# GpSimd makes the temperature features in iterations 1 to 7; VectorE keeps only their reciprocal

## The reference, cut to what matters

```python
qk = jnp.einsum('bhqd,bhkd->bhqk', Q, K)
scores = qk / math.sqrt(dk)
mean_sim = scores.mean(axis=(-2, -1))
max_sim = scores.max(axis=-1).mean(axis=-1)
probs = jax.nn.softmax(scores, axis=-1)
entropy_proxy = jnp.var(probs, axis=-1, ddof=1).mean(axis=-1)
feats = jnp.stack([mean_sim, max_sim, entropy_proxy], axis=-1)
hidden = jax.nn.gelu(_linear(feats, w1, b1), approximate=False)
hidden = jax.nn.gelu(_linear(hidden, w2, b2), approximate=False)
log_t = jnp.clip(_linear(hidden, w3, b3), LOG_T_MIN, LOG_T_MAX)
t = jnp.exp(log_t)[..., None]
attn = jax.nn.softmax(qk / (2.0 * t), axis=-1)
```

## Time and profile before

| | |
|---|---|
| device time, median of three | 1333.83 us (1332.42 to 1334.48) |
| device time of the profiled execution | 1336.35 us |
| its span | 1334.5 us, 23561 instructions |
| PE / DVE / ACT / POOL busy | 1186.8 (89%) / 1093.2 (82%) / 941.7 (71%) / 396.3 us (30%) |
| mean granted clock of TensorE | 0.969 of full speed |

### The profile page before, as it was taken

How to read it: one execution, slowest core, us unless ns; L and a number is a source line. 1 busy time by engine, 2 the same in 40 slices (tenths; PEclk the granted TensorE clock), 3 DMA queues, 4 the chain that set the end, 5 groups by cost and what they waited for, 6 DMA issues and landing times.

```text
span 1334.5 us, 23561 instructions
## 1 busy us (share of the span) xinstructions
PE 1186.8 (89%) x6684; PEld 439.0 (33%) x6684; DVE 1093.2 (82%) x2049; ACT 941.7 (71%) x1593; POOL 396.3 (30%) x387
## 2 busy tenths in 40 slices
PE   4866598989999999998999999999989899869988
PEld 2322221444134422444124431344214441224234
DVE  7789689896998869896998869897898979985256
ACT  4688598576985689575985669665985669765833
POOL 3138555311452024510353124510353101100120
PEclk9969799999999999999999999999999999979989
DMA  8722211221112221211112221102112210001000
GB/s 305 224 75 64 55 41 49 48 48 58 35 39 48 57 74 48 49 38 42 50 48 48 55 76 49 28 21 65 64 49 48 48 65 1 1 0 47 18 0 32
DMA packets 36049, 73.70 MB, mean 55 GB/s; under 512 B 8144, under 2 KB 8528, under 8 KB 35408
## 3 DMA queue, kind: packets, MB, share of 16 engines
q1 hardware_dynamic: 35920, 72.13, 18.8%
HBM read 38.39 MB, written 8.39 MB: 35 GB/s over the span
## 4 chain that ended last, share of the span: by engine, by line
PE 49%; DVE 26%; issue 10%; ACT 8%; SPq 2%; DMA 1%; DVEq 1%; ACTq 0%; POOL 0%; POOLq 0%
PE b_ps L1445 10%; DVE stat L1017 7%; PE o_ps L1685 6%; DVE nmax L1007 5%; PE o_ps L1490 4%; ACT region L810 4%; PE o_ps L1445 4%; PE b_ps L1477 4%; PE a_ps L1471 4%; PE z_ps L1445 3%; ACT etile L778 2%; DVE hmax L1218 2%; PE z_ps L1685 2%; PE z_ps L1501 2%; PE b_ps L1650 2%
## 5 line engine op out<-in xcount | busy, mean ns | idle before, releaser
L778 ACT ACTIVATE etile<-a_ps,nmax 128x512 f32<-128x512 f32 x512 | 369.1, 734 | 104.3 <-DVE nmax L1007 104.1
L810 ACT ACTIVATE region<-b_ps,inv2t 128x512 f32<-128x512 f32 x512 | 354.8, 758 | 50.0 <-PE b_ps L1477 46.1
L1007 DVE TENSOR_REDUCE nmax<-a_ps 128x1 f32<-128x512 f32 x512 | 345.9, 679 | 53.7 <-PE a_ps L1471 49.7
L1017 DVE BATCH_NORM_STATS2 stat<-etile 128x6 f32<-128x512 f32 x492 | 335.5, 685 | 15.5 <-ACT etile L778 15.2
L1471 PE MATMUL a_ps<-kst,qst 96*128 96x512 f16 x512 | 198.1, 390 | 32.1 <-ACT etile L778 25.5
L1477 PE MATMUL b_ps<-qst,kst 97*128 97x512 f16 x512 | 192.8, 389 | 23.6 <-DVE region L1244 7.7
L1490 PE MATMUL o_ps<-region,vbuf 128*32 128x512 f32 x1024 | 137.2, 608 | 10.9 <-ACT region L810 7.1
L1477 PEld LDWEIGHTS b_ps<-qst,kst 97*128 97x128 f16 x512 | 49.2, 96 | 290.4 <-ACT region L810 259.3
L1501 PE MATMUL z_ps<-region,ones 128*32 128x512 f32 x1024 | 136.2, 604 | 8.4 <-DVE region L1054 8.4
L684 POOL TENSOR_TENSOR region<-region 128x512 f16<-128x512 f32 x64 | 79.8, 1249 | 208.9 <-ACT region L851 208.9
L640 POOL TENSOR_TENSOR region<-region 128x512 f32<-128x512 f32 x32 | 40.9, 1280 | 285.4 <-DVE region L1061 285.4
(11 more groups left out here) (313 smaller groups left out, 1989.9 us busy)
## 6 DMA issues: line engine op xcount, KB each, us to landing
kst<-region SPq DMA_DIRECT2D x96, 128.0 KB, 2.3
qst<-region SPq DMA_DIRECT2D x84, 128.0 KB, 2.3
xres<-in_x_dram SPq DMA_DIRECT2D x8, 1024.0 KB, 6.1
out_dram<-xres SPq DMA_DIRECT2D x32, 256.0 KB, 2.0
cin<-in_ctxT_dram SPq DMA_DIRECT2D x30, 256.0 KB, 2.7
cin<-in_x_dram SPq DMA_DIRECT2D x28, 256.0 KB, 2.6
kst<-in_f1T_dram SPq DMA_DIRECT2D x2, 1024.0 KB, 11.5
qst<-in_f2T_dram SPq DMA_DIRECT2D x2, 1024.0 KB, 9.0
```

What stands on the lines that cost most here:

```text
L778: nc.scalar.activation(etile[:, k % E_SLOTS, :], a_ps[k % A_BANKS][:, :], ACT.Exp, bias=nmax[:, slot_of(n), t:t + 1], scale=1.0, accum_out ...
L810: nc.scalar.activation(probs[:, (s + 1) % 2, g, :], b_ps[g % 2][:, :], ACT.Exp, scale=inv2t[:, slot:slot + 1]).then_inc(b_exp, 1)
L1007: vec.tensor_reduce(nmax[:, slot_of(k // T), k % T:k % T + 1], a_ps[k % A_BANKS][:, :], AX.X, ALU.max, negate=True).then_inc(a_max, 1)
L1017: vec.bn_stats(stat[:, slot_of(k // T) * T + k % T, :], etile[:, k % E_SLOTS, :]).then_inc(a_stat, covered)
```

## The change

In bodies with both stage A and stage B (i = 1 to 7) VectorE no longer calls `features`, but `inverse_total`: one wait and the reciprocal. GpSimd makes all else, in three pieces: `feature_products` (two small products, ahead of the four subtractions of Q), `feature_total` (the total and its square, behind a wait for the 64th statistic, ahead of the last subtraction of Q), and `feature_rest` (ten instructions, behind the last subtraction). [...] In iteration 7 GpSimd also does `stats_by_act`, with four instructions in place of three. Iteration 0 stays as it was.

```diff
+            def stats_by_act(i):                      # GpSimd, iteration 7
+                ...
+                pool_waits.wait_ge(squared, BY_ACT[0] + BY_ACT[7])
+                pool.tensor_scalar(mean, mean, 1.0 / S, None, ALU.mult).then_inc(act_pool, 1)
+                pool_waits.wait_ge(act_pool, nth(i, LINKS_ACT, 1))
+                pool.tensor_copy(mean_too, mean)
+                pool.tensor_tensor(rest, mean, mean, ALU.mult).then_inc(act_pool, 1)
+                pool_waits.wait_ge(act_pool, nth(i, LINKS_ACT, 2))
+                pool.tensor_scalar(rest, rest, -float(S), None, ALU.mult).then_inc(act_pool, 1)
+                pool_waits.wait_ge(act_pool, nth(i, LINKS_ACT, 3))
+
+            def feature_products(b, par, c):
+                pool_waits.wait_ge(qk_done, nth(b, 2 * C, 2 * C))
+                c.link(pool.tensor_tensor(qkprod[:, :], qksum[par][:, 0:C], qksum[par][:, C:2 * C], ALU.mult))
+                c.link(pool.tensor_tensor(feat[:, 0, :]..., qkprod..., qmask..., ALU.mult))
+
+            def feature_total(b, c):
+                total = mstep[:, 0, :]
+                pool_waits.wait_ge(a_stat, nth(b, H * T, H * T))
+                if isinstance(b, int) and b == 7:
+                    stats_by_act(b)
+                c.link(pool.tensor_tensor(total, stat[:, :, 1], stat[:, :, 4], ALU.add))
+                c.link(pool.tensor_tensor(total, total, total, ALU.mult))
+
+            def feature_rest(b, c):
+                ...
+                pool_waits.wait_ge(a_max, nth(b, H * T, H * T))
+                c.link(pool.tensor_tensor(some, nmax[:, :, 0:2], nmax[:, :, 2:4], ALU.add))
+                c.link(pool.tensor_tensor(feat[:, 1, :], some[:, :, 0], some[:, :, 1], ALU.add))
+                c.link(pool.tensor_tensor(diff, stat[:, :, 1], stat[:, :, 4], ALU.subtract))
+                c.link(pool.tensor_tensor(diff, diff, diff, ALU.mult))
+                c.link(pool.tensor_scalar(diff, diff, S / 4.0, None, ALU.mult))
+                pool.tensor_tensor(square, stat[:, :, 2], stat[:, :, 5], ALU.add).then_inc(pool_link, 1)
+                ...
+                c.link(pool.tensor_tensor(square, square, diff, ALU.add))
+                pool_waits.wait_ge(inv_done, nth(b, 1, 1))
+                c.link(pool.tensor_tensor(square, square, inv, ALU.mult))
+                c.link(pool.tensor_tensor(some, by_tile[:, :, 0:2], by_tile[:, :, 2:4], ALU.add))
+                pool.tensor_tensor(feat[:, 2, :], some[:, :, 0], some[:, :, 1], ALU.add).then_inc(feat_done, 1)
@@ GpSimd, end of body
-                if has_p:
-                    for n in range(C, 2 * C):
-                        split_qk(n)
+                if has_a and has_b:
+                    c = Chain(pool_waits, pool_link, LINKS_POOL, i)
+                    feature_products(i, par, c)
+                for n in range(C, 2 * C) if has_p else ():
+                    if has_a and has_b and n == 2 * C - 1:
+                        feature_total(i, c)
+                    split_qk(n)
+                if has_a and has_b:
+                    if not has_p:
+                        feature_total(i, c)
+                    feature_rest(i, c)
@@ VectorE
+            def inverse_total(b):
+                dve_waits.wait_ge(pool_link, nth(b, LINKS_POOL, 4))
+                vec.reciprocal(mstep[:, 3, :], mstep[:, 0, :]).then_inc(inv_done, 1)
@@ VectorE, body
-                if has_a and isinstance(i, int) and i == 7:
-                    stats_by_act(i)
-                if has_a:
+                if has_a and has_b:
+                    inverse_total(i)
+                elif has_a:
                     features(i, par)
```

More of the change, by code:

```diff
@@ L71 @@
 LINKS_END = 12
+LINKS_POOL, LINKS_ACT = 13, 3
 LOWEST = -3.0e38
@@ L406, in flamingo_kernel @@
         feat_done = per_batch("feat_done", 1)
+        pool_link, inv_done, act_pool = sem("pool_link"), sem("inv_done"), sem("act_pool")
         logt_done = per_batch("logt_done", 1)
@@ L590, in _ @@
             pool.sem_inc(out_done, 16 * T)
+            pool.sem_inc(pool_link, 2 * LINKS_POOL)
+            pool.sem_inc(inv_done, 2)
+            pool.sem_inc(act_pool, 8 * LINKS_ACT)
             for n in range(UNUSED):
@@ L673, in from_cin @@
                 return cin[:, n % 2, :]
+            def stats_by_act(i):
+                by_tile = stat[:, :, :].rearrange("p (h t) f -> p h t f", t=T)
+                own = by_tile[:, 2 * C - 1::C, :, :]
+                mean, mean_too, rest = (own[:, :, :, f] for f in (1, 4, 5))
+                pool_waits.wait_ge(squared, BY_ACT[0] + BY_ACT[7])
[6 more added lines that the diff above has]
+                pool_waits.wait_ge(act_pool, nth(i, LINKS_ACT, 3))
@@ new lines, in feature_products @@
+            def feature_products(b, par, c):
+                pool_waits.wait_ge(qk_done, nth(b, 2 * C, 2 * C))
+                c.link(pool.tensor_tensor(qkprod[:, :], qksum[par][:, 0:C], qksum[par][:, C:2 * C], ALU.mult))
+                c.link(pool.tensor_tensor(feat[:, 0, :].rearrange("p (g c) -> p g c", g=G4),
+                                          qkprod[:, :].unsqueeze(1).broadcast_to([P, G4, C]),
+                                          qmask[:, :].unsqueeze(2).broadcast_to([P, G4, C]), ALU.mult))
@@ new lines, in feature_total @@
+            def feature_total(b, c):
[6 more added lines that the diff above has]
+            def feature_rest(b, c):
+                total, diff, square, inv = (mstep[:, k, :] for k in range(4))
+                by_tile = square.rearrange("p (h t) -> p h t", t=T)
+                pool_waits.wait_ge(a_max, nth(b, H * T, H * T))
+                some = diff[:, 0:2 * H].rearrange("p (h t) -> p h t", t=2)
+                c.link(pool.tensor_tensor(some, nmax[:, :, 0:2], nmax[:, :, 2:4], ALU.add))
+                c.link(pool.tensor_tensor(feat[:, 1, :], some[:, :, 0], some[:, :, 1], ALU.add))
+                c.link(pool.tensor_tensor(diff, stat[:, :, 1], stat[:, :, 4], ALU.subtract))
+                c.link(pool.tensor_tensor(diff, diff, diff, ALU.mult))
+                pool_waits.stand()
+                c.link(pool.tensor_scalar(diff, diff, S / 4.0, None, ALU.mult))
+                pool.tensor_tensor(square, stat[:, :, 2], stat[:, :, 5], ALU.add).then_inc(pool_link, 1)
+                c.n += 1
+                pool_waits.wait_ge(pool_link, c.base + c.n)
+                c.link(pool.tensor_tensor(square, square, diff, ALU.add))
+                pool_waits.wait_ge(inv_done, nth(b, 1, 1))
+                c.link(pool.tensor_tensor(square, square, inv, ALU.mult))
+                some = total[:, 0:2 * H].rearrange("p (h t) -> p h t", t=2)
+                c.link(pool.tensor_tensor(some, by_tile[:, :, 0:2], by_tile[:, :, 2:4], ALU.add))
+                pool.tensor_tensor(feat[:, 2, :], some[:, :, 0], some[:, :, 1], ALU.add).then_inc(feat_done, 1)
+                c.end()
@@ L1019, in stats_by_act @@
             def stats_by_act(i):
[L1020 to L1025, removed]
+                by_tile = stat[:, :, :].rearrange("p (g c t) f -> p g c t f", g=G4, t=T)
+                own = by_tile[:, :, 1:3, T - 1, :]
                 mean, mean_too, rest = (own[:, :, :, f] for f in (1, 4, 5))
-                links = 2 if i > 0 else 0
-                dve_waits.wait_ge(squared, BY_ACT[0] + (BY_ACT[7] if i > 0 else 0))
+                dve_waits.wait_ge(squared, BY_ACT[0])
                 vec.tensor_scalar(mean, mean, 1.0 / S, None, ALU.mult).then_inc(act_link, 1)
-                dve_waits.wait_ge(act_link, links + 1)
+                dve_waits.wait_ge(act_link, 1)
                 vec.tensor_copy(mean_too, mean)
@@ L1033, in stats_by_act @@
                                          op0=ALU.mult, op1=ALU.mult).then_inc(act_link, 1)
-                dve_waits.wait_ge(act_link, links + 2)
+                dve_waits.wait_ge(act_link, 2)
             def tile_a(b, k, looked=False):
```

## The result

The changed kernel takes 1321.51 us (median of 6, 1319.62 to 1322.55), the kernel before in the same comparison 1332.98 us (1331.44 to 1334.48). The ratio is 0.9913, 95% interval 0.9901 to 0.9925: 11.6 us less (10 to 13). The forecast was 1323.3 us, within 1320.0 to 1328.5. The profiled execution took 1321.19 us with a span of 1319.4 us and the same mean granted clock, 0.969.

A forecast was written before the change was run, and what follows sets the result against it. VectorE's features were taken to hold up the maxima and so TensorE's product. A gain of 12.3 us less 1.8 us paid at the port gives 10.5 us: 1333.83 - 10.5 = 1323.3 us, within 1320 to 1328.5.

The forecast's parts named there:

- What goes from VectorE: Eleven instructions leave VectorE, maxima start at the gelus: 2.07 us in iteration 1, 9.60 in five others, 0.64 in iteration 7.
- The port: VectorE's quantised tile stands behind GpSimd steps at the shared port: 0.3 us in iterations 1 to 6, 1.8 us charged.
- rival (a): Full gain with no collision of VectorE and GpSimd at the port: 12.3 us, 1321.5 us; chance 15%.
- clear range of 1322 to 1326: Total time in the likeliest case, with 0.1 to 0.6 us paid per iteration at the port; 69%.
- Does it pass on whole?: VectorE's 2 us reach TensorE's product at 298.69; `turn(0)` does not stop them, with 0.4 us to spare.
- wait of 1.63 us: TensorE's wait ahead of the fourth product of `up(2)`, claimed to be still there since both sides move.
- Rival (c): The gain is stopped by TensorE's `turn(0)`: 1331.1 to 1332.5 us, 1331.8 as its middle; chance 5%.
- GpSimd: right: Steps of 0.45 us with gaps; total hidden by ScalarE with 0.6 us to spare, the rest with 6 us.
- Rival (d): GpSimd is late with `feat_done`, TensorE's queue stands at the transpose of the maxima: slower, 1346 us; chance 3%.
- Rival (b): VectorE's steps from the tiny ones on stand behind GpSimd steps: 1333.2 us, half as often 1327 us; together 8%.

The follow-up runs named there:

- e2: The kernel before, but GpSimd's last subtraction of Q waits until VectorE's features are done (iterations 1 to 6); 1327.97 us, ratio 0.9965.
- e3: The changed kernel, but GpSimd makes the total and its square behind the last subtraction of Q instead of ahead of it; 1323.70 us, ratio 0.9932.
- e8: The changed kernel with four unused GpSimd additions ahead of the rest of the features, the first 128x256, the others 128x512; 1325.47 us, ratio 0.9939.
- e9: The changed kernel with four unused GpSimd additions ahead of the rest of the features, the first 128x128, the others 128x512; 1322.47 us, ratio 0.9921.
- e7: e4 with VectorE's tiny steps between last maximum and quantised tile cut from five to three, the output's scale made later; 1318.36 us, ratio 0.9888.
- e5: The changed kernel with four unused 128x512 additions on GpSimd ahead of the rest of the features; 1318.57 us, ratio 0.9888.
- e6: The changed kernel with seven unused 128x512 additions on GpSimd ahead of the rest of the features; 1354.54 us, ratio 1.0159.
- e1: The kernel before, but in iterations 1 to 7 VectorE makes the features behind the first quantised tile, not ahead of the first maxima; 1353.71 us, ratio 1.0150.
- e4: The changed kernel, but in iterations 1 to 6 VectorE makes the total and its square itself, the rest stays on GpSimd; 1320.07 us, ratio 0.9904.

## Why the prediction was right

**What goes from VectorE: right.** The maxima start with the first gelu, releaser ScalarE. Computed for iteration 1: 2.07 us, measured 2.07. Computed for the loop's others 1.92; the feature stretch gave 1.91 to 1.93. Taken whole, iterations 2, 4, 5 and 6 gave 1.88, 1.91, 1.81 and 1.92, but 1 and 3 gave 2.69 and 2.22. The surplus lies ahead of the last statistic, where VectorE's work is the same: from the exponential to that statistic's end iteration 1 takes 120.70 us before and 120.07 after, iteration 3 122.49 and 122.20. In iteration 1 it goes with the clock (a mean of 0.71 granted before and 0.82 after, from 6 to 12 us behind the exponential); in iteration 3 the clock is full in both, and the cause stays open. Iteration 7: computed 0.64, measured 0.47, with the clock falling twice in both kernels; e2 and e3 have there the code of before and of after, the first of these falls is in neither, and they differ by 136.13 - 135.47 = 0.66. Computed sum 12.3, measured 11.64 + 0.47 = 12.1 where the change acts, 12.9 by whole iterations of the traces and 11.6 (10 to 13) in the medians.

**The port: the term that was mis-sized.** I charged 0.3 us in each of six iterations for the quantised tile, 1.8 us. Measured 0: its row is 1.28 and 1.29 us as before, and the mean of all 32 is 1286 ns in both kernels. The mechanism exists (e8, e9), but its price is what is left of the GpSimd step less 0.2 us, and the small steps last 0.22 to 0.39 us, so by the same price at worst 0.2 us (an estimate). I had charged nearly the whole of a 0.35 us step; in the loop the tile came with 0.06 to 0.11 us of one left. So the right description is rival (a), full gain, 1321.5 us, and the forecast lay 1.8 us above it; its clear range of 1322 to 1326 just misses the median. That (a) meets the median to 0.01 us is luck: it was counted from 1333.83 us, and the kernel before took 1332.98 beside the changed one. The medians could not even tell 12.3 us from 10.5, since both lie in 10 to 13; the rows do. What the tile does not pay, GpSimd does: one step stands up to 1.0 us behind the first tile of each loop iteration (1.18 instead of 0.22), as the prediction had it, under cover of 6 us.

**Does it pass on whole? Right in the sum, wrong in one picture.** I expected the wait of 1.63 us still to be there, "since both sides move". Only VectorE moves by the whole 2.07 us: TensorE's first three products stood behind `turn(0)`, which came forward by 0.50 us, so the other 1.57 were taken out of that wait, and 0.24 us of it are left. That also says that the gain was nearly all that this wait could give, and e7 shows it: the next 0.64 us taken from VectorE brought just these 0.24. Rival (c) did not come: `turn(0)` was through at 290.26 + 1.06 = 291.32, and the second tile was written from 291.95, 0.6 us later, where 0.4 had been computed.

**GpSimd: right.** Steps of 0.22 to 0.39 us against 0.35, gaps of 0.08 against 0.10. The total was done 0.83 us behind the statistic (1.0 computed), the subtraction started 1.07 us behind it instead of 0.34, 0.7 later as computed, and no one waited for the loads of Q behind it. e3 shows that a reciprocal 1.4 us later costs only 0.4 us an iteration. Rival (d) lay far off: e5 hides 5.8 us more of GpSimd's work, e6 goes past the edge. The steps that read `stat`, six floats apart, take 0.36 to 0.39 us against 0.29 to 0.32 for two packed operands, at most 0.1 more where I had allowed 0.2.

The Trainium skill, "GPSIMD Engine Reference", section "Performance pitfalls for Q7 kernels", states half as much again per element for such a read. These times hold the fixed part of each instruction too, so they agree in the direction and do not test the size.

**Rival (b)** is refuted: the tiny steps of VectorE stay at 0.15 to 0.21 us even beside wide GpSimd steps.

## What to carry to other kernels

Read what is late next before counting what leaves an engine: of 4.38 us of features in iteration 1 2.07 could be gained, and it came to the hundredth, because the gelus' ends bounded it. Then look at what the late engine feeds: TensorE's wait had 0.24 us more to give, and the next saving on VectorE brought no more than that. An idle engine may take such a chain at two times the duration if its result is asked for late, but the two engines' common port is paid by whoever comes second; keep steps on GpSimd short where VectorE has a wide step such as the quantised tile to issue, and look in the trace for which of the two is stretched. Two experiments that show no collision prove nothing if both have the same phase. And measure a small change over the stretch in which it acts: ahead of the feature stretch one iteration differed by up to 1.0 us between the kernels here, whichever edit they had.

## What the runs showed that I had not expected

**A longer wait costs more than itself.** TensorE's wait of 1.63 us is followed by matmuls at full clock, the waits of 3.41 us (e1) and 3.43 us (e6) by about 8 us at a mean granted clock of 0.65 and 0.68. Over the six iterations of the loop such a wait cost 1.3 to 2.4 us beyond its growth in e1 and 1.8 to 2.7 us beyond itself in e6.

**Iteration 7 has a length of its own.** It takes 135.0 us in e5 and 137.35 after, though e5 does more in it. The stretch from 84 to 88 us behind the last exponential of the loop, first after, then e5:

```profile
1153.22:1157.22 4.00, 4.00 (x13) 1.52 (x12) 0.53 (x1) 3.40 (x12) 0.00 (x0) 0.64 0.00 0
```

```profile
1152.70:1156.70 4.00, 4.00 (x20) 1.84 (x19) 1.07 (x2) 3.40 (x12) 0.00 (x0) 1.00 0.00 0
```

TensorE gets through 13 matmuls in one and 20 in the other, by the granted clock of 0.64 and 1.00, ahead of anything that the kernels do differently in that iteration. This fall, between 80 and 88 us behind that exponential, is there in before, after, e4 and e8 and in no other run. These 2.4 us are as large as what several edits here are worth, which is why the loops and the feature stretch decide above and not the medians. What makes the clock fall in one and not in the other was not tried.
